# Pairwise dots on TensorE, one sample or two samples a matmul

## The chip, the cores and the metric

One core of one Trainium2 chip. The metric is the device time of one launch in microseconds (us). PE is the matrix engine TensorE (PEld its weight loads), ACT is ScalarE, DVE is VectorE, POOL is GpSimd, SP is SyncE.

## The reference

A recommendation tower over a batch of 2048. For each sample 26 embedding rows of 128 numbers are looked up in 26 tables and stacked with the sample's dense vector; all 351 pairwise dot products of the 27 vectors are taken, and two hidden layers follow.

```python
e = jnp.stack([tbl_0[ids[:, 0]], ..., tbl_25[ids[:, 25]]], axis=1)
sd = jnp.einsum('bfd,bd->bf', e, dense)
ss = jnp.einsum('bfd,bgd->bfg', e, e)
iu, ju = jnp.triu_indices(26, k=1)
z = jnp.concatenate([dense, sd, ss[:, iu, ju]], axis=1)
h = jnp.concatenate([z, dense], axis=1)
h = jnp.maximum(h @ W_top1 + b_top1, 0.0)
h = jnp.maximum(h @ W_top2 + b_top2, 0.0)
y = h @ W_top3
```

All of it is fp32.

## The kernel before

The batch is cut into 16 tiles of 128 samples, and two tiles are a step. The vectors of a tile are gathered in `vecT`, with the 128 dimensions on the partitions and, along the free axis, 27 numbers for each sample one after another (`vecT[k, slot, s, v]`, three slots). They come in three ways:

- Tables with 1000 rows are looked up on PE: DVE compares ids with row numbers (`set_pack`, L353) and PE multiplies the table by the one-hot matrix in fp32r, in a high and a low part (`lookup`, L599); ACT copies the 128x256 sum into `vecT` (`drain_sum`, L425), two tiles at once.
- The other tables are gathered by POOL with indirect DMAs (L318) into `rows`; PE transposes four vectors at a time (`transpose_rows`, L612) and ACT copies them into `vecT` (`drain_rows`, L433).
- The dense vectors come transposed from memory; ACT copies them in (`copy_x`, L418).

The pairwise dots of a sample are one matmul (`gram`, L626): 26 of its vectors stationary, 26 moving, contracted over the 128 dimensions. The four samples s, s+32, s+64 and s+96 go to output partitions 0, 32, 64 and 96 of one PSUM bank, and 16 such groups fill it (64 matmuls). A tile has two such stretches, h = 0 and 1, each in one of the two `vec_bank` buffers, and ACT copies 128x416 numbers out of each (`drain_gram`, L442) into `dots`. DVE turns `dots` in blocks of 32x32 (`turn`, L363), copies nine trapezoids into `pairs` (L369), PE transposes these (`transpose_pairs`, L640), and ACT copies the result to `pairsT` (L449), on which layer 1 works (L651; its dense part is L647). Layers 2 and 3 are L660 and L666; the last tile has its own order and lines (`last2`, L736; L771; L779).

The order on each engine is written out by hand. On PE a tile of step d stands between lookups of step d + 1 and layer units of step d - 1: Gram stretch, layer unit, one pack of lookup, Gram stretch, layer unit, then the other packs with transposes between them. Semaphores count the fills and drains of a pool: `free_vec(use)` lets PE fill a bank when the fill two uses before is drained. `turn` waits for the drain of a tile's second stretch, POOL's gathers of tile + 2 wait for the tile's last Gram matmul.

```python
s = BL * j + h * HALF + i
last = nc.tensor.matmul(vec_bank[into % 2][BL * j:BL * j + GC, i * GC:(i + 1) * GC],
                        vecT[:, slot(tile), s, 0:GC], vecT[:, slot(tile), s, 1:VECS],
                        start=True, stop=True)
```

Of the kernel before, what the change touches and what calls it, by code (L numbers as in the profile page):

```python
# [16 lines left out]
P = 128  # L17
# [30 lines left out]
def place(v):  # L48
    return order().index(v)
# [9 lines left out]
def build(nc, dense_t, ids, ids_t, tables, weights, y):  # L59
# [28 lines left out]
    HALF = 16  # L88
# [30 lines left out]
    def rows_at(tile, j):  # L119
        return sum(groups(n) + 2 for n in range(tile)) + j  # L120

    def gram_at(tile, h):
        return rows_at(tile, groups(tile)) + h
# [37 lines left out]
    with ctx:  # L161
# [8 lines left out]

        def step_vec(d, v):
            first, second = (vecT[:, slot(TD * d + t), :, v:v + 1] for t in range(TD))
            return bass.AP(first.tensor, first.offset, [first.ap[0], [second.offset - first.offset, TD], [VECS, P]])
# [4 lines left out]
        vecT = sb("vecT", [P, SLOTS, P, VECS])  # L178
# [3 lines left out]
        ids_i = vecT[:, 0, 0:(TWO * DS + VECS - 1) // VECS, :].rearrange("k s v -> k (s v)")[:, 0:TWO * DS].bitcast(i32)  # L182
# [64 lines left out]
        vec_filled, vec_drained = sem("vec_filled"), sem("vec_drained")  # L247
        work_filled, work_drained = sem("work_filled"), sem("work_drained")
# [11 lines left out]
        def _(sp):  # L260
            sp.dma_start(ids_all[:], ids_v).then_inc(ids_loaded, 16)

            sp.dma_start(ids_i, ids_t).then_inc(ids_t_loaded, 16)
# [31 lines left out]
        @block.gpsimd  # L295
        def _(pool):
            nc.gpsimd.memset(ident[:], 0.0).then_inc(ident_zero, 1)
            for c in heights:
                nc.gpsimd.iota(row_i[c][:], pattern=[[1, c]], base=0, channel_multiplier=c
                               ).then_inc(rows_numbered, 1)  # L300
            pool.wait_ge(ident_zero, 1)
            nc.gpsimd.affine_select(out=ident[:], in_=ident[:], compare_op=ALU.not_equal, fill=1.0, base=0,
                                    pattern=[[-1, P]], channel_multiplier=1).then_inc(ident_set, 1)

            pool.wait_ge(ids_loaded, 16)
            for tile in range(TILES):
                for j in range(groups(tile)):
                    if tile >= TD and j == 0:
                        pool.wait_ge(vec_filled, gram_at(tile - TD, 1) + 1)
# [12 lines left out]

        @block.vector
        def _(dve):
            dve.wait_ge(rows_numbered, len(heights))
# [32 lines left out]

            def turn(tile):
                dve.wait_ge(vec_drained, gram_at(tile, 1) + 1)  # L360
# [16 lines left out]
            nc.vector.tensor_copy(idsT[:], ids_i).then_inc(ids_cast, 1)  # L377
# [6 lines left out]
            for tile in range(TILES):  # L384
                d, t = tile // TD, tile % TD
                for k in range(half_packs(d + 1)):
# [4 lines left out]
                    if k == TURN_AFTER:  # L391
                        turn(tile)
# [6 lines left out]
        def _(act):  # L399
# [14 lines left out]
            def copy_x(d):  # L414
                act.wait_ge(x_loaded[d % 2], 16 * (d // 2 + 1))
                if d:
                    act.wait_ge(vec_filled, gram_at(TD * (d - 1), 1) + 1)
                nc.scalar.copy(step_vec(d, place(0)), xT[:, d % 2, :].rearrange("p (t s) -> p t s", t=TD)).then_inc(x_copied, 1)  # L418

            def drain_sum(d, q):  # L420
                use, n = sum_at(d, q), table_at(d, q)
                if q == 0 and d:
                    act.wait_ge(vec_filled, gram_at(TD * (d - 1), 1) + 1)
# [13 lines left out]
            def drain_gram(tile, h):  # L437
                use = gram_at(tile, h)
                if h == 0 and tile:
                    act.wait_ge(tile_turned, tile)  # L440
                act.wait_ge(vec_filled, use + 1)
                nc.scalar.copy(dots[:, h * HALF:(h + 1) * HALF, :],  # L442
                               vec_bank[use % 2][:, 0:HALF * GC].rearrange("p (i f) -> p i f", f=GC)
                               ).then_inc(vec_drained, 1)
# [121 lines left out]
        def _(pe):  # L566
# [49 lines left out]
            def gram(tile, h):  # L616
                into = gram_at(tile, h)
                if h == 0:
                    pe.wait_ge(sum_drained, sum_at(tile // TD + 1, 0))
                    pe.wait_ge(x_copied, tile // TD + 1)  # L620
                    pe.wait_ge(vec_drained, rows_at(tile, groups(tile) - 1) + 1)
                free_vec(into)
# [203 lines left out]
```

## Time and profile before

| | |
|---|---|
| median of 3 runs | 368.81 us (367.7 to 369.45) |
| the profiled execution's own time | 368.79 us |
| its span, first to last instruction | 367.0 us |
| instructions in the span | 13714 |
| mean granted TensorE clock | 0.994 |
| PE busy | 343.3 us, 94% |
| DVE, ACT, POOL busy | 230.8, 188.7, 255.6 us |

The profile shows one execution. A row of a group names the line, the engine, the operation and its tiles (out<-in), the shapes, how often it ran, its busy time, the mean of one, and after the bar the time that the engine was idle just before it, with what ended that. A row of a timeline has the start, the length, the engine and the line; instructions of one kind in a row are one row, with their count. PE's matmuls overlap, so that the length of a row of them reaches over the start of the next row.

### The profile page before, as it was taken

The numbers are of one execution on the slowest core, as the hardware profiler recorded it, in microseconds if no ns is written. First come the engines' busy times: TensorE is split into PE (matmuls) and PEld (weight loads), VectorE is DVE, ScalarE is ACT, GpSimd is POOL, SyncE is SP. The second block draws the span as 40 slices with busy tenths as digits, with TensorE's granted clock in tenths as the row PEclk, the third lists the DMA queues.
The fourth block names the chain that finished last, engine by engine and source line by source line (L and its number), as shares of the span: only waits on it lengthen the run. The fifth ranks groups of instructions, "written<-read, shape, count | busy, mean of one in ns | idle before, by whom it ended". The sixth has DMA issues, their size and how long they took to land.

```text
span 367.0 us, 13714 instructions
## 1 busy us (share of the span) xinstructions
PE 343.3 (94%) x6224; PEld 313.3 (85%) x6224; DVE 230.8 (63%) x324; ACT 188.7 (51%) x283; POOL 255.6 (70%) x273
## 2 busy tenths in 40 slices
PE   1998878999999999999999999999999999999986
PEld 0897777988989898989989898898989889897876
DVE  5799988965839294783929486592938469342030
ACT  1179574553737265553737255362646347372633
POOL 5778777777777777777777777777777777777000
PEclk9999998999999999999999999999999999999999
DMA  7994254222212222212212222212222212212000
GB/s 203 266 233 102 53 172 138 61 53 52 73 54 54 59 66 55 58 53 57 68 54 59 55 67 59 54 52 60 65 54 60 54 52 73 54 53 59 7 5 2
DMA packets 11755, 26.84 MB, mean 73 GB/s; under 512 B 4652, under 2 KB 5804, under 8 KB 11570
## 3 DMA queue, kind: packets, MB, share of 16 engines
q0 software_dynamic: 8512, 17.45, 18.2%
q1 hardware_dynamic: 3186, 8.52, 8.2%
q8 instruction: 49, 0.80, 0.9%
q14 instruction: 8, 0.07, 0.1%
HBM read 25.95 MB, written 0.01 MB: 71 GB/s over the span
## 4 chain that ended last, share of the span: by engine, by line
PE 90%; issue 3%; DVE 2%; DMA 2%; ACT 2%; SPq 0%; DVEq 0%; ACTq 0%
PE sum_bank L599 37%; PE vec_bank L626 14%; PE work L651 10%; PE vec_bank L612 7%; PE work L660 7%; PE work L647 4%; PE sum_bank L595 4%; PE id_bank L573 2%; DMA w_all<-in_tbl 2%; PE work L640 2%; DVE late L363 1%; PE work L666 1%; PE work L736 1%; DVE onehot L353 1%; DVE late L369 1%
## 5 line engine op out<-in xcount | busy, mean ns | idle before, releaser
L318 POOL DMA_INDIRECT rows<-in_tbl,ids_all x266 | 254.8, 958 | 83.3 <-issue 78.6
L353 DVE TENSOR_TENSOR onehot<-id_bank,row_f 125x1024 fp32r<-125x1024 f32 x150 | 174.8, 1217 | 92.0 <-PE sum_bank L599 47.5
L599 PE MATMUL sum_bank<-onehot,parts 125*128 125x256 f32 x1152 | 167.5, 292 | 1.7 <-issue 1.7
L599 PEld LDWEIGHTS sum_bank<-onehot,parts 125*128 125x128 f32 x1152 | 150.6, 192 | 5.7 <-issue 2.3
L433 ACT COPY vecT<-vec_bank 128x512 f32<-128x512 f32 (+1 forms) x74 | 84.9, 1150 | 16.8 <-PE vec_bank L612 16.4
L425 ACT COPY vecT<-sum_bank 128x256 f32<-128x256 f32 x75 | 52.4, 699 | 44.8 <-PE sum_bank L599 28.4
L626 PEld LDWEIGHTS vec_bank<-vecT 128*26 128x26 f32 x4096 | 44.2, 103 | 20.1 <-issue 14.7
L626 PE MATMUL vec_bank<-vecT 128*26 128x26 f32 x4096 | 54.1, 192 | 7.4 <-issue 1.9
L457 ACT ACTIVATE late<-work,w_all 128x256 f32<-128x256 f32 (+1 forms) x50 | 22.8, 458 | 49.6 <-PE work L651 31.4
L442 ACT COPY late<-vec_bank 128x416 f32<-128x416 f32 x32 | 16.2, 506 | 58.6 <-PE vec_bank L626 58.6
L363 DVE STREAM_TRANSPOSE late<-late 128x832 f32<-128x832 f32 x16 | 29.3, 1830 | 25.5 <-ACT late L442 25.5
L651 PE MATMUL work<-late,w_all 126*128 126x256 f32 (+1 forms) x192 | 44.2, 366 | 0.0
L612 PE MATMUL vec_bank<-ident,rows 128*128 128x128 f32 x266 | 41.6, 275 | 0.0
L651 PEld LDWEIGHTS work<-late,w_all 126*128 126x128 f32 x192 | 34.8, 190 | 4.5
L612 PEld LDWEIGHTS vec_bank<-ident,rows 128*128 128x128 f32 x266 | 31.6, 141 | 0.4
L660 PE MATMUL work<-late,w_all 128*128 128x256 f32 x112 | 26.8, 383 | 0.4 <-ACT late L457 0.2
L660 PEld LDWEIGHTS work<-late,w_all 128*128 128x128 f32 x112 | 20.4, 190 | 3.1 <-ACT late L457 0.4
L573 PE MATMUL id_bank<-idsT,pick 128*128 128x512 f32 x38 | 18.5, 492 | 4.6 <-DVE idsT L377 4.6
L647 PE MATMUL work<-xT,w_all 128*128 128x256 f32 (+1 forms) x64 | 19.8, 390 | 0.1
L369 DVE COPY late<-late 128x6 f32<-128x6 f32 (+2 forms) x144 | 16.5, 193 | 1.5
L595 PE MATMUL sum_bank<-onehot,w_all 125*128 125x256 f32 x48 | 13.7, 450 | 3.1 <-DMA w_all<-in_tbl 3.1
L595 PEld LDWEIGHTS sum_bank<-onehot,w_all 125*128 125x128 f32 x48 | 10.9, 232 | 5.8 <-issue 3.8
(40 smaller groups left out, 103.9 us busy)
## 6 DMA issues: line engine op xcount, KB each, us to landing
rows<-in_tbl,ids_all POOLq DMA_INDIRECT x266, 2.6
late<-in_tbl SPq DMA_DIRECT2D x7, 480.0 KB
w_all<-in_weights SPq DMA_DIRECT2D x1, 1571.0 KB, 7.0
w_all<-in_tbl SPq DMA_DIRECT2D x3, 480.0 KB
xT<-in_dense_t SPq DMA_DIRECT2D x8, 128.0 KB
vecT<-in_ids_t SPq DMA_DIRECT2D x1, 256.0 KB, 2.8
late<-in_weights SPq DMA_DIRECT2D x1, 256.0 KB, 7.5
ids_all<-in_ids SPq DMA_DIRECT2D x1, 208.0 KB, 2.5
```

Source lines behind the costliest of these rows:

```text
L318: nc.gpsimd.indirect_dma_start(rows[:, tile % TD, FG * j + n, :], None, tables[f], bass.IndirectOffsetOnAxis(ids_all[:, tile, f:f + 1], 0) ...
L353: nc.vector.tensor_tensor(onehot[:, use % RING, 0:width, :], bass.AP(got.tensor, got.offset, [got.ap[0], [0, width], [1, DS]]), bass.AP(nu ...
L363: nc.vector.transpose(turned.rearrange("p c i -> p (c i)"), dots.rearrange("p i c -> p c i")).then_inc(tile_turned, 1)
L425: nc.scalar.copy(step_vec(d, place(LOOKED_UP[n] + 1)), sum_bank[use % 2][:, 0:DS].rearrange("p (t s) -> p t s", t=TD)).then_inc(sum_draine ...
L433: nc.scalar.copy(vecT[:, slot(tile), :, spot:spot + n].rearrange("d s v -> d v s"), vec_bank[use % 2][:, 0:n * P].rearrange("d (v s) -> d ...
L595: last = nc.tensor.matmul(into_sum, uncut[n - SPLIT_AT_FIRST][:, (c0 + c) * DIM:(c0 + c + 1) * DIM], hot.bitcast(fp32), start=first, stop= ...
L599: last = nc.tensor.matmul(into_sum, parts[:, k, CH_AT[n] + c0 + c, :], hot, start=first and k == 0, stop=final and k == PARTS - 1)
L612: last = nc.tensor.transpose(vec_bank[into % 2][:, n * P:(n + 1) * P], rows[:, tile % TD, FG * j + n, :], ident[:])
L626: last = nc.tensor.matmul(vec_bank[into % 2][BL * j:BL * j + GC, i * GC:(i + 1) * GC], vecT[:, slot(tile), s, 0:GC], vecT[:, slot(tile), s ...
L647: nc.tensor.matmul(out, w1x[:, cols], xT[:, d % 2, s0:s0 + ns], start=True, stop=False)
L651: last = nc.tensor.matmul(out, w1p[:, b, cols], pairsT[0:KP, b, s0:s0 + ns], start=False, stop=(b == KT - 1))
L660: last = nc.tensor.matmul(work_bank[use % 2][:, 0:ns], w2_sb[:, b, m * P:(m + 1) * P], h1[:, b, s0:s0 + ns], start=(b == 0), stop=(b == M1 ...
```

## The change

Two neighbouring samples of `vecT` share a matmul. Samples lie 32 places apart instead of 27, the five places between are set to zero once, and the stationary operand is two whole samples, 64 columns; the moving one is the 26 needed places of both, 52 columns. The product is 64x52: the dots of the first sample are its upper left 32x26 block, those of the second the lower right one, and the other two blocks are not used. Output partitions 0 to 63 and 64 to 127 take turns. A tile now has four fills of 16 matmuls (FILL = 8 for each half of the partitions), two in each of the old stretches. ACT takes a fill out with one copy of all 128 partitions, right for the first samples, and then two copies of 32 partitions that put the second samples' dots over what is wrong (in the last tile DVE makes the latter). So that dots end up at the sample's old place, the ids are put in another order before the launch, and the copy of the dense vectors orders them alike, now in two copies. The ids for the one-hots get a buffer of their own.

```diff
-    HALF = 16
+    FILLS = 4
+    FILL = 8
+    SPAN = 32
...
+        def dots_of(use, second):
+            bank = vec_bank[use % 2][:, 0:FILL * 2 * GC].rearrange("p (i m f) -> p m i f", m=2, f=GC)
+            return bank[:, second, :, :]
...
-        vecT = sb("vecT", [P, SLOTS, P, VECS])
+        vecT = sb("vecT", [P, SLOTS, P, SPAN])
...
+            nc.vector.memset(vecT[:, :, :, VECS:SPAN], 0.0).then_inc(pad_set, 1)
...
+            def copy_last_seconds():
+                for f in range(FILLS):
+                    use = gram_at(TILES - 1, f)
+                    dve.wait_ge(firsts_copied, FILLS * (TILES - 1) + f + 1)
+                    for q in (BL, 3 * BL):
+                        last = nc.vector.tensor_copy(dots[q:q + BL, f * FILL:(f + 1) * FILL, :],
+                                                     dots_of(use, 1)[q:q + BL])
+                    last.then_inc(vec_drained, 1)
+
             def turn(tile):
-                dve.wait_ge(vec_drained, gram_at(tile, 1) + 1)
+                dve.wait_ge(vec_drained, gram_end(tile))
...
-                nc.scalar.copy(step_vec(d, place(0)), xT[:, d % 2, :].rearrange("p (t s) -> p t s", t=TD)).then_inc(x_copied, 1)
+                for t in range(TD):
+                    into = vecT[:, slot(TD * d + t), :, place(0)]
+                    last = nc.scalar.copy(into.rearrange("k (g i m) -> k g i m", g=2, m=2),
+                                          xT[:, d % 2, t * P:(t + 1) * P].rearrange("k (g m i) -> k g i m", g=2, m=2))
+                last.then_inc(x_copied, 1)
...
-                act.wait_ge(vec_filled, use + 1)
-                nc.scalar.copy(dots[:, h * HALF:(h + 1) * HALF, :],
-                               vec_bank[use % 2][:, 0:HALF * GC].rearrange("p (i f) -> p i f", f=GC)
-                               ).then_inc(vec_drained, 1)
+                for f in fills:
+                    use = gram_at(tile, f)
+                    act.wait_ge(vec_filled, use + 1)
+                    nc.scalar.copy(dots[:, f * FILL:(f + 1) * FILL, :], dots_of(use, 0)).then_inc(firsts_copied, 1)
+                for f in fills if tile < TILES - 1 else ():
+                    use = gram_at(tile, f)
+                    act.wait_ge(firsts_copied, FILLS * tile + f + 1)
+                    for q in (BL, 3 * BL):
+                        last = nc.scalar.copy(dots[q:q + BL, f * FILL:(f + 1) * FILL, :], dots_of(use, 1)[q:q + BL])
+                    last.then_inc(vec_drained, 1)
...
-                for i in range(HALF):
-                    for j in range(4):
-                        s = BL * j + h * HALF + i
-                        last = nc.tensor.matmul(vec_bank[into % 2][BL * j:BL * j + GC, i * GC:(i + 1) * GC],
-                                                vecT[:, slot(tile), s, 0:GC], vecT[:, slot(tile), s, 1:VECS],
-                                                start=True, stop=True)
-                last.then_inc(vec_filled, 1)
+                for f in range(FILLS // 2 * h, FILLS // 2 * (h + 1)):
+                    into = gram_at(tile, f)
+                    free_vec(into)
+                    for i in range(FILL):
+                        for g in range(2):
+                            s = 2 * (BL * g + f * FILL + i)
+                            last = nc.tensor.matmul(
+                                vec_bank[into % 2][2 * BL * g:2 * BL * (g + 1), 2 * i * GC:2 * (i + 1) * GC],
+                                vecT[:, slot(tile), s:s + 2, :].rearrange("k s v -> k (s v)"),
+                                vecT[:, slot(tile), s:s + 2, 1:VECS], start=True, stop=True)
+                    last.then_inc(vec_filled, 1)
...
+    ids = ids.reshape(2, 2, 32, TILES, FEATS).transpose(0, 2, 1, 3, 4).reshape(BATCH, FEATS)
```

On PE, in the middle of the program, where the first tile of a step is at its Gram stretches between units of layers 1 and 3 and a pack of lookup, before:

```order
L651 MATMUL work<-late,w_all 128x256 x3
L626 MATMUL vec_bank<-vecT 26x26 x64
L647 MATMUL work<-xT,w_all 128x256
L651 MATMUL work<-late,w_all 128x256 x3
L599 MATMUL sum_bank<-onehot,parts 128x256 x8
L626 MATMUL vec_bank<-vecT 26x26 x64
L647 MATMUL work<-xT,w_all 128x256
L651 MATMUL work<-late,w_all 128x256 x3
L599 MATMUL sum_bank<-onehot,parts 128x256 x16
```

and now:

```order
L687 MATMUL work<-late,w_all 128x256 x3
L661 MATMUL vec_bank<-vecT 64x52 x32
L683 MATMUL work<-xT,w_all 128x256
L687 MATMUL work<-late,w_all 128x256 x3
L631 MATMUL sum_bank<-onehot,parts 128x256 x8
L661 MATMUL vec_bank<-vecT 64x52 x32
L683 MATMUL work<-xT,w_all 128x256
L687 MATMUL work<-late,w_all 128x256 x3
L631 MATMUL sum_bank<-onehot,parts 128x256 x16
```

Nothing stands in another place; a stretch of 64 matmuls of 26x26 is one of 32 matmuls of 64x52 (two fills of 16, which follow each other). The new numbers of the lines are 661 for the Gram, 683 and 687 for layer 1, 631 for the lookup.

On ACT, around the two stretches of a tile, before (L442 is the Gram's copy, L457 an activation of a layer, L468 the copy of y, L425 and L433 the copies into `vecT`):

```order
L457 ACTIVATE late<-work,w_all 128x256
L442 COPY late<-vec_bank 128x416
L457 ACTIVATE late<-work,w_all 128x256
L425 COPY vecT<-sum_bank 128x256
L442 COPY late<-vec_bank 128x416
L468 COPY y_lines<-work 128x2x32
L425 COPY vecT<-sum_bank 128x256
L433 COPY vecT<-vec_bank 128x4x128
```

and now (L470 and L475 are the Gram's copies, L489 the activation, L500 y, L451 and L459 into `vecT`):

```order
L489 ACTIVATE late<-work,w_all 128x256
L470 COPY late<-vec_bank 128x208 x2
L475 COPY late<-vec_bank 32x208 x4
L489 ACTIVATE late<-work,w_all 128x256
L451 COPY vecT<-sum_bank 128x2x128
L470 COPY late<-vec_bank 128x208 x2
L475 COPY late<-vec_bank 32x208 x4
L500 COPY y_lines<-work 128x2x32
L451 COPY vecT<-sum_bank 128x2x128
L459 COPY vecT<-vec_bank 128x4x128
```

Six copies stand where one stood, ahead of the activation and of the copies of sums that were queued behind it.

On DVE, at the end of the program, before:

```order
L353 TENSOR_TENSOR onehot<-id_bank,row_f 125x1024 x2
L363 STREAM_TRANSPOSE late<-late 128x832
L369 COPY late<-late 128x6
L369 COPY late<-late 128x15
...
L369 COPY late<-late 128x78
L363 STREAM_TRANSPOSE late<-late 128x832
L369 COPY late<-late 128x6
```

and now:

```order
L364 TENSOR_TENSOR onehot<-id_bank,row_f 125x1024 x2
L383 STREAM_TRANSPOSE late<-late 128x832
L389 COPY late<-late 128x6
L389 COPY late<-late 128x15
...
L389 COPY late<-late 128x78
L375 COPY late<-vec_bank 32x208 x8
L383 STREAM_TRANSPOSE late<-late 128x832
L389 COPY late<-late 128x6
```

Eight copies of 32x208 have come between the last two rounds of transpose and trapezoids, ahead of the last transpose (L363 before, L383 now).

## Rows read from the trace of the kernel before

**Rows 1.** The page's parts 1 and 2: busy shares; the clock in 40 slices.
```profile
PE 343.3 (94%) x6224; PEld 313.3 (85%) x6224; DVE 230.8 (63%) x324; ACT 188.7 (51%) x283; POOL 255.6 (70%) x273
...
PEclk9999998999999999999999999999999999999999
```
**Rows 2.** The page's part 4: the chain that ended last, by line.
```profile
PE sum_bank L599 37%; PE vec_bank L626 14%; PE work L651 10%; PE vec_bank L612 7%; PE work L660 7%; PE work L647 4%; PE sum_bank L595 4%; PE id_bank L573 2%; DMA w_all<-in_tbl 2%; PE work L640 2%; DVE late L363 1%; PE work L666 1%; PE work L736 1%; DVE onehot L353 1%; DVE late L369 1%
```
**Rows 3.** Groups by form, PE and PEld: busy us, mean ns | idle before, releasers.
```profile
L626 PE MATMUL vec_bank<-vecT 128*26 128x26 f32 x4096 | 54.1, 192 | 7.4 <-issue 1.9 <-ACT vecT L433 1.2 <-ACT vecT L425 0.8
...
L626 PEld LDWEIGHTS vec_bank<-vecT 128*26 128x26 f32 x4096 | 44.2, 103 | 20.1 <-issue 14.7 <-ACT vecT L425 1.0
...
L736 PEld LDWEIGHTS work<-late,w_all 128*128 128x128 f32 x32 | 3.9, 192 | 0.4 <-issue 0.3
```
**Rows 4.** Timeline of PE, a tile in the middle: start us, us, instructions.
```profile
142.41 1.80 PE L626 MATMUL vec_bank<-vecT 128*26 128x26 f32 x128
...
144.14 1.99 PE L660 MATMUL work<-late,w_all 128*128 128x256 f32 x8
...
147.02 1.77 PE L626 MATMUL vec_bank<-vecT 128*26 128x26 f32 x126
```
**Rows 5.** Timeline of PE, the last tile's two stretches.
```profile
348.91 1.26 PE L626 MATMUL vec_bank<-vecT 128*26 128x26 f32 x128 [0.21 <-ACT vecT L433]
...
350.10 0.49 PE L647 MATMUL work<-xT,w_all 128*128 128x128 f32 x2
...
352.33 1.12 PE L626 MATMUL vec_bank<-vecT 128*26 128x26 f32 x111 [0.83 <-issue]
```
**Rows 6.** Timeline of PE, 142.41 to 142.60 alone.
```profile
142.41 0.37 PE L626 MATMUL vec_bank<-vecT 128*26 128x26 f32 x25
```
**Rows 7.** Timeline of PE, weights of 128 columns, near the end.
```profile
340.79 3.69 PE L660 MATMUL work<-late,w_all 128*128 128x256 f32 x16 [0.22 <-ACT late L457]
...
344.32 0.60 PE L612 MATMUL vec_bank<-ident,rows 128*128 128x128 f32 x4
...
357.00 0.55 PE L640 MATMUL work<-ident,late 128*126 128x128 f32 x3 [0.27 <-DVE late L369]
...
357.39 1.06 PE L736 MATMUL work<-late,w_all 128*128 128x128 f32 x8
...
358.28 1.50 PE L779 MATMUL sum_bank<-late,w_all 126*128 126x128 f32 x12
```
**Rows 8.** Groups of ACT, the page's part 5, and the 32-column form.
```profile
L433 ACT COPY vecT<-vec_bank 128x512 f32<-128x512 f32 (+1 forms) x74 | 84.9, 1150 | 16.8 <-PE vec_bank L612 16.4
L425 ACT COPY vecT<-sum_bank 128x256 f32<-128x256 f32 x75 | 52.4, 699 | 44.8 <-PE sum_bank L599 28.4
...
L442 ACT COPY late<-vec_bank 128x416 f32<-128x416 f32 x32 | 16.2, 506 | 58.6 <-PE vec_bank L626 58.6
...
L468 ACT COPY y_lines<-work 128x32 f32<-128x32 f32 x2 | 0.4, 213 | 0.4 <-PE work L666 0.4
```
**Rows 9.** Timeline of ACT behind the second stretch of a middle tile.
```profile
149.47 0.51 ACT L442 COPY late<-vec_bank 128x416 f32<-128x416 f32 x1 [2.82 <-PE vec_bank L626]
...
150.50 0.70 ACT L425 COPY vecT<-sum_bank 128x256 f32<-128x256 f32 x1 [0.34 <-PE sum_bank L599]
...
151.89 1.22 ACT L433 COPY vecT<-vec_bank 128x512 f32<-128x512 f32 x1 [0.70 <-PE vec_bank L612]
```
**Rows 10.** Timeline of DVE at the start and in a middle tile; groups of DVE.
```profile
4.00 0.43 DVE L377 CAST idsT<-vecT 128x512 fp32r<-128x512 int32 x1 [2.39 <-DMA vecT<-in_ids_t]
...
151.64 1.88 DVE L363 STREAM_TRANSPOSE late<-late 128x832 f32<-128x832 f32 x1
...
L363 DVE STREAM_TRANSPOSE late<-late 128x832 f32<-128x832 f32 x16 | 29.3, 1830 | 25.5 <-ACT late L442 25.5
...
L369 DVE COPY late<-late 128x78 f32<-128x78 f32 x16 | 3.6, 222 | 0.0
...
L369 DVE COPY late<-late 128x24 f32<-128x24 f32 x16 | 2.7, 171 | 0.0
```

More of the change, by code:

```diff
@@ L119, in rows_at, with gram_at, gram_end @@
     def rows_at(tile, j):
-        return sum(groups(n) + 2 for n in range(tile)) + j
-    def gram_at(tile, h):
-        return rows_at(tile, groups(tile)) + h
+        return sum(groups(n) + FILLS for n in range(tile)) + j
+    def gram_at(tile, f):
+        return rows_at(tile, groups(tile)) + f
+    def gram_end(tile):
+        return gram_at(tile, FILLS - 1) + 1
     def same_rows(tile, j):
@@ L169, in sem @@
             return ctx.enter_context(nc.semaphore(name))
+        def dots_of(use, second):
+            bank = vec_bank[use % 2][:, 0:FILL * 2 * GC].rearrange("p (i m f) -> p m i f", m=2, f=GC)
+            return bank[:, second, :, :]
         def step_vec(d, v):
             first, second = (vecT[:, slot(TD * d + t), :, v:v + 1] for t in range(TD))
-            return bass.AP(first.tensor, first.offset, [first.ap[0], [second.offset - first.offset, TD], [VECS, P]])
+            return bass.AP(first.tensor, first.offset, [first.ap[0], [second.offset - first.offset, TD], [SPAN, P]])
         ids_all = sb("ids_all", [P, TILES, FEATS], i32)
@@ L181, in build @@
         idsT = sb("idsT", [P, TWO * DS], fp32r)
-        ids_i = vecT[:, 0, 0:(TWO * DS + VECS - 1) // VECS, :].rearrange("k s v -> k (s v)")[:, 0:TWO * DS].bitcast(i32)
+        ids_i = sb("ids_i", [P, TWO * DS], i32)
         y_lines = sb("y_lines", [P, BL * TILES])
@@ L247, in build @@
         vec_filled, vec_drained = sem("vec_filled"), sem("vec_drained")
+        pad_set, firsts_copied = sem("pad_set"), sem("firsts_copied")
         work_filled, work_drained = sem("work_filled"), sem("work_drained")
@@ L261, in _ @@
             sp.dma_start(ids_all[:], ids_v).then_inc(ids_loaded, 16)
-            sp.dma_start(ids_i, ids_t).then_inc(ids_t_loaded, 16)
+            sp.dma_start(ids_i[:], ids_t).then_inc(ids_t_loaded, 16)
             def load_table(n, dst, loaded):
@@ L308, in _ @@
                     if tile >= TD and j == 0:
-                        pool.wait_ge(vec_filled, gram_at(tile - TD, 1) + 1)
+                        pool.wait_ge(vec_filled, gram_end(tile - TD))
                     if tile >= TD and j == SECOND_HALF_FROM:
@@ L376, in _ @@
             dve.wait_ge(ids_t_loaded, 16)
-            nc.vector.tensor_copy(idsT[:], ids_i).then_inc(ids_cast, 1)
+            nc.vector.tensor_copy(idsT[:], ids_i[:]).then_inc(ids_cast, 1)
             dve.wait_ge(row_f_set, len(heights))
@@ L391, in _ @@
                     if k == TURN_AFTER:
+                        if tile == TILES - 1:
+                            copy_last_seconds()
                         turn(tile)
@@ L416, in copy_x @@
                 if d:
-                    act.wait_ge(vec_filled, gram_at(TD * (d - 1), 1) + 1)
-                nc.scalar.copy(step_vec(d, place(0)), xT[:, d % 2, :].rearrange("p (t s) -> p t s", t=TD)).then_inc(x_copied, 1)
+                    act.wait_ge(vec_filled, gram_end(TD * (d - 1)))
+                for t in range(TD):
[3 more added lines that the diff above has]
+                last.then_inc(x_copied, 1)
             def drain_sum(d, q):
@@ L422, in drain_sum @@
                 if q == 0 and d:
-                    act.wait_ge(vec_filled, gram_at(TD * (d - 1), 1) + 1)
+                    act.wait_ge(vec_filled, gram_end(TD * (d - 1)))
                 act.wait_ge(pack_done, PER * use + PER)
@@ L437, in drain_gram @@
             def drain_gram(tile, h):
-                use = gram_at(tile, h)
+                fills = range(FILLS // 2 * h, FILLS // 2 * (h + 1))
                 if h == 0 and tile:
                     act.wait_ge(tile_turned, tile)
-                act.wait_ge(vec_filled, use + 1)
-                nc.scalar.copy(dots[:, h * HALF:(h + 1) * HALF, :],
-                               vec_bank[use % 2][:, 0:HALF * GC].rearrange("p (i f) -> p i f", f=GC)
-                               ).then_inc(vec_drained, 1)
+                for f in fills:
[8 more added lines that the diff above has]
+                    last.then_inc(vec_drained, 1)
             def drain_pairs(tile):
@@ L616, in gram @@
             def gram(tile, h):
-                into = gram_at(tile, h)
                 if h == 0:
+                    if tile == 0:
+                        pe.wait_ge(pad_set, 1)
                     pe.wait_ge(sum_drained, sum_at(tile // TD + 1, 0))
```

1 line of the change is left out of this document (removed).

## The prediction

> **What bounds the kernel now.** I read the busy shares and the clock first, then the chain that ended last, then the Gram's own stretches. TensorE is busy 94% of the span, at a granted clock of 9 tenths or more in nearly every slice, its higher level of 2.4 GHz [rows 1]. The chain that ended last names the Gram line, L626, with 14% of the span, all of it as PE's own work [rows 2]. PE hardly waits there: 1.2 and 0.8 us, for ACT [rows 3]. So a microsecond taken from PE or given to it is one of the kernel's, and work on ACT, DVE or POOL counts only where it gets late enough for PE to wait.
>
> The Gram costs PE 54.1 us of busy time, with 7.4 us of idle time before its records, 2.0 of them the waits for ACT [rows 3]. It comes in 32 stretches of 128 matmul records (64 matmuls of 26 stationary by 26 moving columns, two passes each for fp32). A usual one lasts from 142.41 to 144.14, 1.73 us; the first of the last tile from 348.91 to 350.10, 1.19 us [rows 4, 5]. The rows of the latter end at 350.17, and a record lasts 0.19, so its last one starts 0.12 before the next operation, and 128 starts fill 1.07 us: 8.4 ns a record. For all 32: 54.1 + 5.4 of idle inside, less the 0.07 of each last record that lies beyond the next start (2.3), is 57.2 us, **1.79 us a stretch**.
>
> What limits a stretch? The one at 348.91 has no pause. The one behind it stops for 0.83 us with "issue" as the cause [rows 5], and the weight loads of L626 were idle 14.7 us on issue in all [rows 3]. So PE gets these small instructions more slowly than it runs them, with pauses. In the first 0.19 us of a stretch, fed from what was queued, 25 records begin, 7.6 ns each [rows 6]. Four blocks of 32 output partitions take turns there, so one block takes 30 ns for a record.
>
> **The PE part of the change.** The records are halved to 64 a stretch, but each loads 64 columns and moves 52, and there are two blocks of 64. Columns have a price of their own. With 256 moving columns 16 records take 340.79 to 344.32, 220 ns each; with 128 moving and 128 stationary 8 records take 357.39 to 358.28, 111 ns [rows 7]: 0.87 ns a moving column. Weight loads last 103 ns for 26 columns and 192 for 128 [rows 3], 0.87 ns a stationary column. As 128 and 128 take 111 and not 222, load and move of neighbouring records overlap and the longer one counts. In a 64-wide block that is the load: 64 x 0.87 = 55.5 ns, against 52 x 0.87 = 45 for the move. The fixed part on top is 0 by the row with 128 columns, and 7.5 ns by the 26-column row (30 against 22.5). I take 57 ns, nearer to the wider row, which is bound by columns as this is. Two blocks in turns: 28.5 ns per record, 1.82 us for 64, and 0.12 until the next operation starts, as now. That is 1.94 us a stretch. Pauses on issue are covered, since PE would take an instruction every 14 ns, and the pauseless stretch was fed one every 4.2. **32 x 1.94 - 57.2 = +5.0 us.** With 55.5 and 63 ns in place of 57: +3.5 and +11.
>
> The Trainium skill speaks against this step: TensorEngine Tiling (Array Packing), Instruction Overhead, says that each matmul has about 60 cycles of overhead, so that one column costs what 60 do. By that rule 52 columns would cost what 26 do, and the sum would lose nearly half of the Gram, to some 341 us. The trace doesn't bear it out for these operands: a moving column took 0.87 ns, two cycles, which puts 52 columns beyond such a floor.
>
> **The ACT part.** Now one copy of 416 columns a stretch, 506 ns; one of 32 columns costs 213 [rows 8]: 0.76 ns a column, 347 ns for 208. After: two copies of 128x208 and four of 32x208 a stretch, the latter behind a wait for the former. I price the narrow ones like the wide ones; 213 ns is their lower end. A queued ACT copy leaves room for the next 0.1 us before its end, so 0.25 each in a row. Behind the last matmul of a stretch come one wide and four narrow copies and some 0.15 for the wait: 1.4 us, now 0.5. ACT's busy time grows by 64 + 120 copies of 0.35 less 15.7: 48 us, to some 237 of 367, and it waited 58.6 us before just these copies [rows 8]. Place by place: behind the copy at 149.47 the sum's copy would move from 150.50 to some 151.3, and the one at 151.89 would be on time again [rows 9]. DVE's transpose starts at 151.64 behind its own one-hots [rows 10]; the drain would be done near 151.0. POOL's gathers wait for the Gram's end, and not for the drain. So the ACT part costs **0**. If the cover were gone, a drain that is 0.9 us late in each tile would cost 14 us; that is the upper end.
>
> The copy of x becomes two of 128 columns, in time that is idle on ACT: 0. The fills wait for banks drained two uses earlier; between the second and the third PE has from 144.14 to 147.02 for other work [rows 4], the copies need 1.4: 0. The gathers fetch as many rows, in another order: 0. The memset on DVE has 1,920 elements. A DVE copy of 24 columns took 171 ns and one of 78 took 222, 0.94 a column; the transpose took 2.2 an element (1830 for 832) [rows 10]. So it lasts 1.8 to 4.2 us. DVE is idle for 2.39 us before 4.00, where the ids land [rows 10]: 0, at worst 1.8.
>
> **The end.** In the last tile DVE copies the second samples. From the last Gram record on, ACT needs 0.35 in place of 0.51, and DVE two copies of 208 columns before it can transpose: 171 + 184 x 0.94 = 345 ns for one, about 0.6 for both. PE already waits for DVE's result there, 0.27 us before 357.00 [rows 7]. So this lies on the path: **+0.5 us** (0.35 + 0.6 - 0.51).
>
> **Sum.** The profiled execution took 368.8 us (span 367.0), and the median of three is 368.81, the same number. 368.8 + 5.0 + 0.5 = **374.3 us**. A measurement of this kernel can tell about 0.5%, 1.8 us, from no change.
>
> **Rivals.**
> - *The move alone counts.* Loads go so far ahead of the moves that their length drops out. For it: with 256 moving columns a load of 128 is hidden whole. 45 / 2 = 22.5 ns a record, 1.56 us a stretch, -7.3 in all: **362 us**. Chance 0.18.
> - *Instructions set the pace*, as they do now, and there are half as many: 64 x 8.4 ns + 0.12 + one pause of 0.25 is 0.91 us, -28: **341 us**. For it: the pauses. Against it: 0.87 ns a column. Chance 0.10. The rule on overhead would end here.
> - *The two halves of the array do not work side by side.* Blocks of 32 are seen to; no row shows one of 64. Above 26 ns a record the Gram gets slower; here it is 57: 3.77 us a stretch, +63: **433 us**. Chance 0.06.
> - *ACT becomes the bound.* Samples in vecT lie 128 bytes apart, not 108, and copies into it are dear already (699 ns for 256 columns, against 506 for 416 that lie together [rows 8]). If the distance doubled them again, 84.9 + 52.4 us more and the 48 from above make some 374 us of work, and with ACT's waits at the start and end some **395 us**. Up to a third more would be hidden. No row speaks for it. Chance 0.08.
> - The forecast, with 26 to 32 ns a record, has 0.52. The last 0.06 is for a gain and a loss elsewhere that leave the time where it is.
>
> **How the numbers follow.** Faster: 0.18 + 0.10 = 0.28. Within 0.5%: the forecast's part below 26.7 ns a record (0.10) and the 0.06 make 0.16. Slower: 0.42 + 0.06 + 0.08 = 0.56. The forecast's own range is 369 to 382 us. The range for 8 in 10 leaves out the two far cases, 341 and 433, with 0.16 together: 360 to 396.
>
> **What would show it.** Right: 64 Gram records a stretch of some 1.9 us, 28 ns apart with no pause on issue; weight loads of about 136 ns (103 + 38 x 0.87); PE still busy 93% or more; no wait of PE for ACT beyond those of now. Wrong: records less than 25 ns apart (first and second rival), over 50 (third), or copies into vecT that last half as long again, with PE waiting for them (fourth).

## The result, and the profile after

The changed kernel took 376.43 us in the median (375.72 to 378.57), the kernel before, measured beside it, 368.25 (367.31 to 369.45). The ratio is 1.0211, 95% interval 1.0177 to 1.0246: +8.2 us where +5.5 was forecast, and inside the range.

| | before | after | after, second profile |
|---|---|---|---|
| the profiled execution's span | 367.0 us | 376.7 us | 374.2 us |
| instructions | 13714 | 9787 | 9787 |
| PE busy | 343.3 us | 358.2 us | 355.7 us |
| ACT busy | 188.7 us | 223.3 us | 222.8 us |
| granted TensorE clock | 0.994 | 0.982 | 0.990 |

The page of the changed kernel: busy shares, the clock in 40 slices, the chain by line [before: rows 1, 2].

```profile
PE 358.2 (95%) x4176; PEld 334.1 (89%) x4176; DVE 234.6 (62%) x333; ACT 223.3 (59%) x443; POOL 256.9 (68%) x273
...
PEclk9998995999999999999999999999999999999999
...
PE sum_bank L631 34%; PE vec_bank L661 17%; PE work L687 10%; PE vec_bank L644 7%; PE work L696 7%; PE work L683 4%; POOL rows L328 4%; DMA rows<-in_tbl,ids_all 2%; PE id_bank L605 2%; PE work L676 2%; DVE late L383 1%; PE work L702 1%; PE work L772 1%; DMA ids_all<-in_ids 1%; DVE onehot L364 1%
```

The Gram's share of the chain has grown from 14% to 17%, with half the records. POOL's gathers and their DMA now stand at the chain's start, since PE waits 2.0 us for them at L644 in the second profile (2.3 in the first, nothing before the change). The first Gram stretch begins no later for it: at 39.47 us there and at 39.55 before. The seventh clock slice stands out with its 5. A row of the timeline and a window say what it is:

```profile
62.40 3.64 PE L661 MATMUL vec_bank<-vecT 128*64 128x52 f32 x64 [0.66 <-ACT vecT L459]
```

```profile
60.00:66.00 6.00, 5.34 (x74) 0.51 0.23 59
```

(The window's columns: length, PE busy and records, granted clock, DMA share, GB/s.) In this execution the clock stood at its lower level, 1.2 GHz, through one whole Gram stretch and the work before it (granted 0.56 from 55 to 60 us, 0.51 from 60 to 66), after PE had waited 2.6 us for DVE; the stretch took 3.57 us to the next operation at 65.97. In a second profile of the same kernel it was back at the higher level by 60 us (0.66 from 55 to 60, then 1.00), as it was in the kernel before (0.66, then 1.00), so I read the rest there. Its Gram groups, and both stretches of a middle tile [before: rows 3, 4]:

```profile
L661 PE MATMUL vec_bank<-vecT 128*64 128x52 f32 x2048 | 66.4, 222 | 1.6 <-ACT vecT L459 0.8 <-issue 0.7
...
L661 PEld LDWEIGHTS vec_bank<-vecT 128*64 128x64 f32 x2048 | 62.4, 138 | 8.8 <-issue 6.4 <-ACT late L475 0.5
```

```profile
144.84 2.08 PE L661 MATMUL vec_bank<-vecT 128*64 128x52 f32 x64
146.84 1.99 PE L696 MATMUL work<-late,w_all 128*128 128x256 f32 x8
...
149.71 2.08 PE L661 MATMUL vec_bank<-vecT 128*64 128x52 f32 x64
151.72 0.43 PE L702 MATMUL work<-late,w_all 128*32 128x64 f32 x16
```

Both stretches last 2.00 us, and the rest of the 32 the same within 10 ns: the pauses on issue are gone (1.6 us of idle time in all, 7.4 before). The last record starts 0.15 us before the next operation (146.92 less 0.22 is 146.70, against 146.84), so 66.4 us busy less 32 x 0.07 is 64.1 us, against 57.2: **the Gram is 7 us dearer**. Where the rest is, three places of the span tell. They are the starts of the first, fifth and twenty-ninth stretch, before and then in the second profile:

```profile
39.55 1.81 PE L626 MATMUL vec_bank<-vecT 128*26 128x26 f32 x128 [0.76 <-ACT vecT L425]
...
78.14 1.82 PE L626 MATMUL vec_bank<-vecT 128*26 128x26 f32 x128
...
330.80 1.94 PE L626 MATMUL vec_bank<-vecT 128*26 128x26 f32 x128
```

```profile
39.47 2.08 PE L661 MATMUL vec_bank<-vecT 128*64 128x52 f32 x64 [0.73 <-issue]
...
79.03 2.08 PE L661 MATMUL vec_bank<-vecT 128*64 128x52 f32 x64
...
337.15 2.08 PE L661 MATMUL vec_bank<-vecT 128*64 128x52 f32 x64
```

From the fifth to the twenty-ninth: 252.66 and 258.12 us, +5.5 for 24 stretches. Before the fifth +0.9, behind the twenty-ninth +0.85 (36.2 and 37.05 us). Together 7.2, the difference of the spans. The medians are 8.2 us apart, and 6.7 when both kernels were measured once more (375.83 against 369.09): 7.2 lies between the two.

### The profile page after: what moved, and what is told of

It is laid out like the page before. It is cut to its first block, busy times and chain, and to the rows that moved or that the text cites. A ratio compares the mean times of both kernels' runs of the same rounds, so it can differ in the third digit from the quotient of the medians.

```text
span 376.7 us, 9787 instructions
## 1 busy us (share of the span) xinstructions
PE 358.2 (95%) x4176; PEld 334.1 (89%) x4176; DVE 234.6 (62%) x333; ACT 223.3 (59%) x443; POOL 256.9 (68%) x273
## 4 chain that ended last, share of the span: by engine, by line
PE 85%; POOL 4%; DMA 3%; ACT 3%; issue 2%; DVE 2%; DVEq 0%
PE sum_bank L631 34%; PE vec_bank L661 17%; PE work L687 10%; PE vec_bank L644 7%; PE work L696 7%; PE work L683 4%; POOL rows L328 4%; DMA rows<-in_tbl,ids_all 2%; PE id_bank L605 2%; PE work L676 2%; DVE late L383 1%; PE work L702 1%; PE work L772 1%; DMA ids_all<-in_ids 1%; DVE onehot L364 1%
## 5 line engine op out<-in xcount | busy, mean ns | idle before, releaser
L459 ACT COPY vecT<-vec_bank 128x512 f32<-128x512 f32 (+1 forms) x74 | 76.2, 1032 | 20.2 <-PE vec_bank L644 20.2
L661 PEld LDWEIGHTS vec_bank<-vecT 128*64 128x64 f32 x2048 | 63.9, 141 | 8.8 <-issue 6.4
L661 PE MATMUL vec_bank<-vecT 128*64 128x52 f32 x2048 | 68.0, 225 | 1.4 <-issue 0.7
L451 ACT COPY vecT<-sum_bank 128x256 f32<-128x256 f32 x75 | 47.2, 629 | 37.1 <-PE sum_bank L631 22.5
L470 ACT COPY late<-vec_bank 128x208 f32<-128x208 f32 x64 | 21.2, 333 | 47.4 <-PE vec_bank L661 43.0
L644 PE MATMUL vec_bank<-ident,rows 128*128 128x128 f32 x266 | 42.3, 278 | 2.3 <-DMA rows<-in_tbl,ids_all 2.3
L489 ACT ACTIVATE late<-work,w_all 128x256 f32<-128x256 f32 (+1 forms) x50 | 22.9, 458 | 33.4 <-PE work L687 19.9
L475 ACT COPY late<-vec_bank 32x208 f32<-32x208 f32 x120 | 38.9, 324 | 2.2
L383 DVE STREAM_TRANSPOSE late<-late 128x832 f32<-128x832 f32 x16 | 29.2, 1825 | 13.0 <-ACT late L475 13.0
L644 PEld LDWEIGHTS vec_bank<-ident,rows 128*128 128x128 f32 x266 | 31.8, 142 | 2.9 <-DMA rows<-in_tbl,ids_all 2.5
L627 PE MATMUL sum_bank<-onehot,w_all 125*128 125x256 f32 x48 | 12.4, 416 | 2.6 <-DMA w_all<-in_tbl 2.6
```

Of the source, the lines that this page charges most:

```text
L383: nc.vector.transpose(turned.rearrange("p c i -> p (c i)"), dots.rearrange("p i c -> p c i")).then_inc(tile_turned, 1)
L451: nc.scalar.copy(step_vec(d, place(LOOKED_UP[n] + 1)), sum_bank[use % 2][:, 0:DS].rearrange("p (t s) -> p t s", t=TD)).then_inc(sum_draine ...
L459: nc.scalar.copy(vecT[:, slot(tile), :, spot:spot + n].rearrange("d s v -> d v s"), vec_bank[use % 2][:, 0:n * P].rearrange("d (v s) -> d ...
L475: last = nc.scalar.copy(dots[q:q + BL, f * FILL:(f + 1) * FILL, :], dots_of(use, 1)[q:q + BL])
L644: last = nc.tensor.transpose(vec_bank[into % 2][:, n * P:(n + 1) * P], rows[:, tile % TD, FG * j + n, :], ident[:])
L661: last = nc.tensor.matmul(vec_bank[into % 2][2 * BL * g:2 * BL * (g + 1), 2 * i * GC:2 * (i + 1) * GC], vecT[:, slot(tile), s:s + 2, :].re ...
```

## The experiments

**58 stationary columns.**

```diff
-    vec_bank[into % 2][2 * BL * g:2 * BL * (g + 1), 2 * i * GC:2 * (i + 1) * GC],
-    vecT[:, slot(tile), s:s + 2, :].rearrange("k s v -> k (s v)"),
+    vec_bank[into % 2][2 * BL * g:2 * BL * g + SPAN + GC, 2 * i * GC:2 * (i + 1) * GC],
+    vecT[:, slot(tile), s:s + 2, :].rearrange("k s v -> k (s v)")[:, 0:SPAN + GC],
```

> The changed kernel with 58 stationary columns in place of 64 (the six zeros behind the second sample are not loaded); the 52 moving ones stay. In the changed kernel's trace records come in pairs, one in each half of the array, 58.3 ns apart, 32 pairs a stretch. If the weight load sets that distance (theory LOAD), it falls by 6 x 0.83 = 5 ns to 53.3, a stretch from 2.005 to 1.84 us, and the kernel from 376.4 to about 371. If the 52 moving columns (MOVE) or a fixed price of a record in a 64-wide block (FIXED) set it, the distance stays 58.3 and the time within 0.5 us.

371.68 us, 1.0069 of before (1.0044 to 1.0094). A stretch:

```profile
144.08 1.92 PE L661 MATMUL vec_bank<-vecT 128*58 128x52 f32 x64
145.92 1.99 PE L696 MATMUL work<-late,w_all 128*128 128x256 f32 x8
```

1.84 us against 2.00: 0.16 / 32 is 5 ns for six columns, 0.83 a column, as LOAD says. Even so it is above the kernel before.

**26 moving columns.**

```diff
-    vec_bank[into % 2][2 * BL * g:2 * BL * (g + 1), 2 * i * GC:2 * (i + 1) * GC],
+    vec_bank[into % 2][2 * BL * g:2 * BL * (g + 1), 2 * i * GC:(2 * i + 1) * GC],
...
-    vecT[:, slot(tile), s:s + 2, 1:VECS], start=True, stop=True)
+    vecT[:, slot(tile), s, 1:VECS], start=True, stop=True)
```

> The changed kernel with 26 moving columns, those of the first sample alone; the 64 stationary ones stay. The dots of the second samples are left out, and their places hold what was there. LOAD: pairs stay 58.3 ns apart, time within 1 us of the changed kernel's 376.4. MOVE: the distance falls to about 30 ns and the kernel by 32 x 32 x 28 ns = 29 us. FIXED: as LOAD.

375.07 us, 1.0174 (1.0128 to 1.0221).

```profile
143.68 2.05 PE L661 MATMUL vec_bank<-vecT 128*64 128x26 f32 x64
145.67 1.99 PE L696 MATMUL work<-late,w_all 128*128 128x256 f32 x8
```

Half of the moving columns gone, and a stretch is 1.99 us: MOVE has fallen. FIXED fell with the run before. The time is 1.4 us below 376.4, a little more than the 1 us expected; the 32 stretches give 0.7 of it, and the changed kernel itself came out at 375.83 when measured once more.

**104 moving columns.**

```diff
+    both = vecT[:, slot(tile), s:s + 2, 1:VECS]
...
-    vec_bank[into % 2][2 * BL * g:2 * BL * (g + 1), 2 * i * GC:2 * (i + 1) * GC],
+    vec_bank[into % 2][2 * BL * g:2 * BL * (g + 1), 2 * i * GC:2 * (i + 2) * GC],
...
-    vecT[:, slot(tile), s:s + 2, 1:VECS], start=True, stop=True)
+    bass.AP(both.tensor, both.offset, [both.ap[0], [0, 2]] + list(both.ap[1:])),
```

> The changed kernel with 104 moving columns (both samples' 26 twice; the second half lands where the next matmul writes over it). 64 stationary as before. If load and move of neighbouring records overlap and the longer one counts, 104 x 0.83 + 5 = 92 ns from pair to pair in place of 58.3: 32 x 32 x 33.5 ns = +34 us, about 411. If the move never counts beside the load: no change. If both add up with what is there now (MOVE): 52 more columns, +43 ns a pair, +44 us, about 421.

405.53 us, 1.1007 (1.0989 to 1.1026).

```profile
131.92 3.07 PE L662 MATMUL vec_bank<-vecT 128*64 128x104 f32 x64
134.92 0.70 PE L685 MATMUL work<-xT,w_all 128*128 128x256 f32 x2
```

3.00 us: a pair every 89.2 ns by the starts of its records, 31 ns more, where 104 x 0.83 + 5 would give 33. The time is some 5 us below the expected 411, 2 of them in the stretches (32 x 1.00 in place of 34). Against the second profile the other 3 lie ahead of the fifth stretch: the first begins at 37.07 us and not at 39.47, and from 30 to 35 us the clock was granted at 1.00 here and at 0.74 there. From the fifth stretch on the 1.00 a stretch is all that is added. Load and move overlap, and the longer one counts.

**Samples 32 places apart alone.**

```diff
-        vecT = sb("vecT", [P, SLOTS, P, VECS])
+        vecT = sb("vecT", [P, SLOTS, P, SPAN])
...
-    [second.offset - first.offset, TD], [VECS, P]]
+    [second.offset - first.offset, TD], [SPAN, P]]
...
+        ids_i = sb("ids_i", [P, TWO * DS], i32)
...
```

> The kernel before with samples 32 places apart in vecT and a buffer of its own for the ids, and nothing else of the change: one sample a matmul, 26 by 26. It tells the price of the new distance alone. I expect ACT's copies into vecT shorter, as in the changed kernel (1125 in place of 1252 ns for 512 columns, 629 in place of 699 for 256), and the time the same as before, 368 within 1 us, since ACT is covered. Rival: the distance of 128 bytes slows PE's reads and part of the 8 us is its: then stretches over 1.79 us and up to 376.

368.52 us, 0.9990 (0.9975 to 1.0005). ACT's copies into `vecT` [before: rows 8]:

```profile
L434 ACT COPY vecT<-vec_bank 128x512 f32<-128x512 f32 x64 | 71.8, 1125 | 18.6 <-PE vec_bank L613 18.6
L426 ACT COPY vecT<-sum_bank 128x256 f32<-128x256 f32 x75 | 47.2, 629 | 46.9 <-PE sum_bank L600 31.0 <-PE sum_bank L596 14.9
```

They are 10% shorter than the 1252 and 699 ns of before, and it gives nothing back, since ACT is covered. No part of the 8 us is the distance's.

**32 stationary columns, one sample a matmul** (from the same form, with the zeros loaded too).

```diff
-    vec_bank[into % 2][BL * j:BL * j + GC, i * GC:(i + 1) * GC],
-    vecT[:, slot(tile), s, 0:GC], vecT[:, slot(tile), s, 1:VECS],
+    vec_bank[into % 2][BL * j:BL * (j + 1), i * GC:(i + 1) * GC],
+    vecT[:, slot(tile), s, 0:SPAN], vecT[:, slot(tile), s, 1:VECS],
```

> The kernel before with samples 32 places apart, and 32 stationary columns in place of 26 (the zeros are loaded too); 26 moving. In the queued part of a stretch four records, one in each quarter, take 26.7 ns; by LOAD that becomes 32 x 0.83 + 5 = 31.7. Fed from memory, four records take 33.5. So if the supply of instructions is what limits the kernel before (theory PACE), 6 more columns cost next to nothing: 8 groups of four in each stretch are 5 ns longer, +1.3 us in all, 369 to 370. If columns limited it, every group of four would grow by 5 ns: 32 x 32 x 5 = +5 us, 373.

368.10 us, 0.9970 (0.9947 to 0.9993). Six more columns in 4,096 loads cost nothing that the time shows, where in the changed kernel six columns in 2,048 loads gave back 5 us. By the starts of the records, groups of four in the queued part of a stretch now take 32 ns (26.7 before), and those behind it 33.5 as before; the 32 stretches fill 57.1 us against 57.0. Before the change columns were free; after it they are the price. That is PACE.

**Each stretch in two, with a layer unit between.**

```diff
-            def gram(tile, h):
+            def gram(tile, h, part=None):
...
-                for i in range(HALF):
+                for i in range(half * (part == 1), HALF - half * (part == 0)):
...
-                    gram(tile, h)
+                    gram(tile, h, 0 if d else None)
...
+                    if d:
+                        gram(tile, h, 1)
```

> The kernel before with each Gram stretch cut in two (32 matmuls each) and the layer unit that stood behind it put between, from the second step on up to tile 13; the order on the other engines stays. PACE says that 17 us of the Gram's 57 are pauses, since PE drains its queue of instructions in a long stretch. While a unit of long matmuls runs, the queue fills. Expected by PACE: most pauses gone in 24 of 32 stretches, -0.5 us each, against one more entry and exit of the small blocks (0.1 + 0.1 us): -0.3 x 24 = -7 us, 361. If pauses come with the number of instructions whatever stands between (a pause for each block fetched), they only move: +0.2 x 24 = +5 us, 373.

368.10 us, 0.9975 (0.9953 to 0.9997); -7 us was expected. The two halves that answer to the stretch at 142.41 [rows 4]:

```profile
141.96 0.87 PE L628 MATMUL vec_bank<-vecT 128*26 128x26 f32 x64
142.76 1.99 PE L663 MATMUL work<-late,w_all 128*128 128x256 f32 x8
144.69 0.92 PE L628 MATMUL vec_bank<-vecT 128*26 128x26 f32 x64
145.54 1.21 PE L599 MATMUL sum_bank<-onehot,parts 125*128 125x256 f32 x8
```

0.80 + 0.85 is 1.65 us in place of 1.73, so less than 0.1 of the 0.5 us of pauses is saved net. Over the 24 stretches in the middle the kernel took 253.5 us, 0.9 more than before: the Gram's own records fill 39.2 us in place of 42.0, and the layer units between them 4.4 more. Nor did the pauses go. The weight loads of the Gram were idle 14.7 us on issue before [before: rows 3]; here:

```profile
L628 PEld LDWEIGHTS vec_bank<-vecT 128*26 128x26 f32 x4096 | 44.4, 103 | 22.8 <-issue 17.0
```

So neither expectation was met, not the -7 and not the +5 us: splitting doesn't take the pauses away. What sets their number is open.

**Without ACT's second-sample copies in tiles 0 to 14.**

```diff
...
-                for f in fills if tile < TILES - 1 else ():
-                    use = gram_at(tile, f)
-                    act.wait_ge(firsts_copied, FILLS * tile + f + 1)
-                    for q in (BL, 3 * BL):
-                        last = nc.scalar.copy(dots[q:q + BL, f * FILL:(f + 1) * FILL, :], dots_of(use, 1)[q:q + BL])
-                    last.then_inc(vec_drained, 1)
...
```

> The changed kernel without ACT's 120 copies of second samples in tiles 0 to 14 (those dots are left out); the last tile stays as it is. The forecast put the ACT part at 0: time the same as the changed kernel's 376.4, within 0.7 us. Rival: the late drains cost PE somewhere between 1 and 14 us, and the time falls by that.

373.44 us, 1.0115 (1.0082 to 1.0148): 0.9% less than the changed kernel's 1.0211, where nothing was expected. Against the 1.0166 (1.0118 to 1.0214) that the changed kernel gave when measured once more the intervals overlap, so the timelines have to decide. The starts of the first, fifth and twenty-ninth stretch:

```profile
38.32 2.08 PE L656 MATMUL vec_bank<-vecT 128*64 128x52 f32 x64 [0.73 <-issue]
...
76.31 2.08 PE L656 MATMUL vec_bank<-vecT 128*64 128x52 f32 x64
...
334.51 2.08 PE L656 MATMUL vec_bank<-vecT 128*64 128x52 f32 x64
```

From the fifth on it is 258.20 us, as with the copies (258.12): there they are free, as forecast. The gain is all in front, 39.47 less 38.32 us ahead of the first stretch and 39.6 less 38.0 from the first to the fifth. The first part, 1.15 us, can't come from the copies, which begin behind the first stretch; there the clock was granted at 0.74 from 30 to 35 us with them and at 1.00 without. In the second part ACT splits the last tables and DVE waits for it. DVE's waits, in the second profile with the copies:

```profile
DVE parts L349 <- ACT parts L428: 2.4, 2, 1.4
DVE parts L349 <- ACT work L434: 2.0, 2, 1.4
```

and without them:

```profile
DVE parts L349 <- ACT parts L428: 1.4, 1, 1.4
...
DVE parts L349 <- ACT work L434: 0.4, 1, 0.4
```

4.4 us against 1.8, and 2.1 before the change (1.5 and 0.6 at L338). DVE then turns tile 0's dots later, and PE waits for them. Where that wait ends, before the change, in the second profile, and without the copies:

```profile
55.29 0.75 PE L640 MATMUL work<-ident,late 128*126 128x128 f32 x3 [2.59 <-DVE late L369]
```

```profile
56.07 0.76 PE L676 MATMUL work<-ident,late 128*126 128x128 f32 x3 [2.58 <-DVE late L389]
```

```profile
53.82 0.55 PE L671 MATMUL work<-ident,late 128*126 128x128 f32 x3 [2.56 <-DVE late L389]
```

From the start of the first stretch that is 15.74, 16.60 and 15.50 us. In all three the clock was granted at 1.00 from the first stretch to 55 us, so the copies alone cost PE 1.1 us here, 0.9 against the kernel before. Behind it, from 55 to 60 us, the clock was granted at 0.66 with the copies and at 1.00 without, and the way to the fifth stretch took 23.0 and 22.5 us: what is left for the clock is half a microsecond.

**Without DVE's eight copies at the end.**

```diff
-                        if tile == TILES - 1:
-                            copy_last_seconds()
...
```

> The changed kernel without DVE's eight copies of second samples in the last tile (those dots are left out in that tile). The forecast put the end at +0.5 us: PE's wait for the last trapezoids gets shorter by 0.5 to 0.6 us, and the time falls by as much, within noise of the changed kernel. Rival: the copies are covered by PE's own work and nothing moves.

375.41 us, 1.0183 (1.0152 to 1.0215). The time can't show half a microsecond; the timeline does. The last Gram stretch's successor and PE's wait for the trapezoids, with the copies (second profile) and without:

```profile
360.43 0.49 PE L683 MATMUL work<-xT,w_all 128*128 128x128 f32 x2
...
364.67 0.55 PE L676 MATMUL work<-ident,late 128*126 128x128 f32 x3 [1.30 <-DVE late L389]
```

```profile
360.16 0.49 PE L682 MATMUL work<-xT,w_all 128*128 128x128 f32 x2
...
363.60 0.55 PE L675 MATMUL work<-ident,late 128*126 128x128 f32 x3 [0.50 <-DVE late L389]
```

4.24 us against 3.44: the copies cost 0.8. Before the change it was 3.62 (353.38 to 357.00), so against the kernel before the end costs +0.6.

**Both matmuls in one half.**

```diff
-    vec_bank[into % 2][2 * BL * g:2 * BL * (g + 1), 2 * i * GC:2 * (i + 1) * GC],
+    vec_bank[into % 2][0:2 * BL, 2 * i * GC:2 * (i + 1) * GC],
```

> The changed kernel with both matmuls of a group put out to partitions 0 to 63, one after the other; partitions 64 to 127 get nothing, so the dots are those of half of the samples. SIDE BY SIDE (the forecast): records in the two halves of the array overlap in the changed kernel, and here no longer: 58.3 ns for each of 64 records, a stretch of 3.88 us in place of 2.005, +60 us, about 436. Rival: the pairs 7 ns apart are the two passes of one matmul and the halves take turns anyway: stretches stay at 2.0 us.

432.47 us, 1.1721 (1.1663 to 1.1778).

```profile
134.27 3.94 PE L661 MATMUL vec_bank<-vecT 128*64 128x52 f32 x64
138.14 0.70 PE L683 MATMUL work<-xT,w_all 128*128 128x256 f32 x2
```

3.87 us a stretch: without the other half every record costs 58 ns (436 us was expected). So in the changed kernel the halves do work side by side, and this is what the third rival would have looked like.

**Blocks of 64 and of 32 mixed** (54 matmuls a stretch).

```diff
+                for i in range(MIXED):
+                    s, c = h * 64 + 6 * i, i % 8 * 2 * GC
+                    nc.tensor.matmul(vec_bank[into % 2][0:SPAN + GC, c:c + 2 * GC],
...
+                    for n in range(4):
+                        q, c = 2 + n % 2, i % 8 * 2 * GC + n // 2 * GC
...
-                for i in range(HALF):
+                for i in range(15, HALF):
...
```

> A look for a form that beats both. The kernel before with samples 32 places apart; in each stretch ten groups of six samples: one matmul of 58 by 52 columns for two samples in partitions 0 to 57, and four of 26 by 26 in the blocks at 64 and 96, then four samples as before: 54 matmuls in place of 64. Places in dots are not sorted out, so the output is scrambled; only the time counts. If blocks of 64 and of 32 work side by side, a group takes 2 x 53.5 ns for six samples, 1.07 us for ten and some 1.3 a stretch against 1.79; with the pauses gone -0.45 x 32 = -14 us, 354; with the pauses as they are about 0, 368. If the sizes exclude each other (a change of block size empties the array), each group pays two changes of some 0.1 us and the time goes over 410.

464.68 us in the median; the ratio, 1.2492 (1.2381 to 1.2602), is that of the executions at 464.18 and 457.68, since the others spent longer at the lower clock. From 140 to 160 us, where the rows below stand, it was granted at 1.00.

```profile
149.94 0.31 PE L631 MATMUL vec_bank<-vecT 128*58 128x52 f32 x2
150.18 0.29 PE L636 MATMUL vec_bank<-vecT 128*26 128x26 f32 x8
150.40 0.31 PE L631 MATMUL vec_bank<-vecT 128*58 128x52 f32 x2
```

A group of six samples takes 0.46 us, not 0.11. The second 58-column record starts 0.09 us behind the first, and the small ones 0.15 behind it, so the two sorts don't run side by side: a change of block size has to wait.

**The changed kernel once more, and the two small edits together** (samples 32 apart, split stretches).

> The changed kernel once more, for a second profile: in the first one the clock was granted at half in the stretch at 62 us, which then took 3.57 us. Expected: with the clock full there, span about 374, 32 Gram stretches of 2.005 us (64.2 in all), the part from the fifth stretch to the twenty-ninth 258.1 us as before; time 375 to 376. If the first profile was typical, a long stretch shows up again and the span is 376 or more.

375.83 us, 1.0166 (1.0118 to 1.0214), with the span and stretches expected.

> The kernel before with samples 32 places apart and with each Gram stretch cut in two around a layer unit, the two edits that came out a little below the kernel before (0.9990 and 0.9975 of it). If both are real and add up: 0.9965, 367 us. More likely neither is over 0.5%: 0.996 to 1.001.

368.89 us, 0.9982 (0.9959 to 1.0005): neither is worth anything that this measurement can tell. No form that was run is clearly faster than the kernel before.

## Why the prediction was right

- *The limit before.* Right: instructions came too slowly (6 more columns a load were free). One reading was coarse: the 7.6 ns a record of the queued part [rows 6] average in one gap of 28 ns behind the first four; the others start 6.7 ns apart, 26.7 a group of four and not 30. The groups behind them take 33.5 ns, so that the supply of instructions, and not the columns, set their pace.
- *The rule on overhead.* The forecast would have come out at 341 us if 64 by 52 columns had cost what 26 by 26 do. 26 moving columns did cost what 52 do (1.99 against 2.00 us a stretch), but because the load of 64 was the longer part; six stationary columns less gave back 0.16 us a stretch. So the forecast's argument against the rule, the price of a moving column, was not what decided: it was the stationary side, of which the rule in the Trainium skill (TensorEngine Tiling (Array Packing), Instruction Overhead) says nothing. Whether moving columns alone have such a floor no run here shows.
- *The Gram after.* The mechanism was right and its size a little low: 1.94 us a stretch forecast, 2.005 measured. The pair's distance was 58.3 ns and not 57, with one longer step at the start (92 ns from the first pair to the second): the last record starts 1.86 us after the first, 1.82 was forecast. From there to the next operation it is 0.15 us and not 0.12. Over 32 stretches 7.0 us in place of 5.0. The weight load lasted 138 ns, 136 was forecast.
- *ACT at 0.* Right from the second step on. Missed in the first tile: my place-by-place reading took a tile in the middle, and at the start ACT still splits tables that DVE waits for. That is 0.9 us at the full clock, between the first stretch and tile 0's trapezoids. The wide and narrow copies took 332 and 323 ns; 347 was forecast. But narrow ones in a row don't overlap as I took them to (0.25 each): four took 1.34 us. In a middle tile the drain is done 1.8 us behind the stretch (146.84 to 148.66) and not 1.4, and the cover holds even so. ACT's busy time came to 223 us and not 237, mostly since its copies into `vecT` got 13 us shorter.

```profile
147.32 1.34 ACT L475 COPY late<-vec_bank 32x208 f32<-32x208 f32 x4
```

- *The end.* +0.5 forecast, +0.6 measured: two DVE copies took 0.76 us and not 0.6.
- *The sum.* 7.0 + 0.9 + 0.6 is 8.5, and the spans are 7.2 apart: 1.3 us were gained elsewhere. 0.5 of that is in the middle, where the 24 stretches are 6.0 us longer and the kernel 5.5; the rest lies mostly behind the twenty-ninth stretch. What it comes from I did not follow. So the total being close to the forecast owes something to terms that cancel. Rivals one to three are excluded by the runs, the fourth by the copies into `vecT` having become shorter.

## What to carry to other kernels

Packing more work into a matmul saves instructions, not columns: work out the array's time per block, the longer of stationary and moving columns at 0.83 ns each and a few ns, before counting instructions. Widening a block from 32 to 64 halves the number of blocks at work: four samples take one period of a block (from one record in it to the next) either way, so the period has to get shorter for the packing to gain. Here it was 33.5 ns, or some 52 with the pauses (1.79 us less 0.12 over 32 groups), set by the supply of instructions, and became 58.3, set by the load; at 58 stationary columns it is 53.3, still too long. Zeros loaded for alignment are paid in full where the load is the longer part. When work is added to a covered engine, look for the cover in the first tile too, not only in the steady state.

## What the hardware showed that I had not expected

- ACT's copies with one element per sample got faster with 128 bytes between them than with 108: 1125 against 1252 ns for 512 columns, 629 against 699 for 256.
- The same expression, columns times 0.83 plus 5 ns, fits the period of a block under stationary loads of 26, 32, 58 and 64 columns (26.7, 32, 53.3 and 58.3 ns; the first two while fed from the queue). With 104 moving columns it is 89.2 ns, 104 x 0.83 plus some 2.5.
- A group with records of both 64-wide and 32-wide blocks took 0.46 us, where side by side they would need 0.11. It has two changes of width, so by my estimate a change costs 0.18 us.
- One wait of 2.6 us by PE for DVE was followed in one execution by the lower clock through a whole Gram stretch (3.57 us in place of 2.0); in another of the same kernel, behind a wait as long, it was at the higher level again before the stretch began.
